# GpSimd's four-tap convolution in operations of 256 columns, two halves of each step in turn, on one Trainium2 core

## What is computed

```python
x = x + xattn(layernorm(x), ctx)            # one head over 8192 context rows, softmax
x = x + linear_attn(layernorm(x))           # 16 heads, relu features, rms norms
x = x + ffn(layernorm(x))
# ffn(h), h of 512 x 512
scores = sigmoid(h @ Wr)                    # router, 8 experts, the best 2 of scores + router_bias
cw = weights of the two chosen, normalised, zero elsewhere
hid = silu(h @ Wg[e]) * (h @ Wu[e])         # e = 0..3, 256 hidden columns each
routed = sum_e cw[:, e] * (hid @ Wd[e]) + (cw[:, 4] + cw[:, 6]) * h + cw[:, 7] * relu(h)
shared[t] = conv_b + sum_j conv_w[3 - j] * h[t - j]      # j = 0..3, per feature, causal
return routed + shared
```

## Time and profile before

| | |
|---|---|
| median of 3 runs | 528.38 us (528.27 to 528.65) |
| the profiled execution | 528.52 us, its span 526.4 us |
| outside the span | 2.1 us |
| granted TensorE clock | 0.999 of full speed |
| busy: PE, PEld | 521.2 us (99%), 433.2 us (82%) |
| busy: DVE, ACT, POOL | 373.4 us (71%), 243.8 us (46%), 244.1 us (46%) |
| the convolution on POOL | 464.8 to 517.2 us, 32 operations |

### The profile page before, as it was taken

The page is one execution under the profiler, slowest core; times in us unless marked ns, Lnnn a source line. Parts: engine busy times, 40 slices in busy tenths (PEclk is TensorE's granted clock), DMA queues, the critical chain, the costliest instruction groups (busy, mean ns, idle before and its releaser), DMA issues.

```text
span 526.4 us, 6975 instructions
## 1 busy us (share of the span) xinstructions
PE 521.2 (99%) x2524; PEld 433.2 (82%) x2524; DVE 373.4 (71%) x620; ACT 243.8 (46%) x391; POOL 244.1 (46%) x159
## 2 busy tenths in 40 slices
PE   9999999999999999999999999999999999999997
PEld 8888888888888888888888888888888888888785
DVE  5573768866668776466878544999967367649995
ACT  5743434745445454453545444656555332562210
POOL 3725006331211312234144342348529939897992
PEclk9999999999999999999999999999999999999999
DMA  8821223332422233422332212242340304741102
GB/s 290 331 69 52 80 95 106 113 127 82 158 82 80 81 105 136 157 85 80 122 119 80 82 40 82 80 161 90 113 157 1 127 34 136 244 162 60 60 1 80
DMA packets 17607, 57.10 MB, mean 108 GB/s; under 512 B 2083, under 2 KB 2595, under 8 KB 16806
## 3 DMA queue, kind: packets, MB, share of 16 engines
q1 hardware_dynamic: 17430, 56.53, 30.6%
q10 hardware_dynamic: 144, 0.13, 0.1%
HBM read 54.55 MB, written 2.10 MB: 108 GB/s over the span
## 4 chain that ended last, share of the span: by engine, by line
PE 95%; DVE 3%; issue 1%; ACT 0%; POOL 0%; DVEq 0%; POOLq 0%
PE bank L1459 24%; PE bank L1577 11%; PE bank L1588 11%; PE bank L1578 11%; PE bank L1589 11%; PE bank L1590 11%; PE bank L1579 11%; PE bank L1509 2%; PE bank L1449 1%; DVE tied L1362 1%; PE bank L1718 1%; PE bank L1470 1%; DVE xs L1398 1%; PE bank L1484 0%; DVE hid_l L1384 0%
## 5 line engine op out<-in xcount | busy, mean ns | idle before, releaser
L576 POOL TENSOR_TENSOR cn_l<-raw_n,cn_h 128x1024 fp32r<-128x1024 f32 x32 | 77.7, 2427 | 185.5 <-ACT cn_h L758 185.5
L776 ACT COPY ring<-bank 128x512 f32<-128x512 f32 x64 | 37.7, 589 | 148.3 <-PE bank L1579 148.0
L1093 DVE TENSOR_TENSOR top<-top,bank 128x512 f32<-128x512 f32 x60 | 41.1, 686 | 86.3 <-ACT ring L776 86.3
L1577 PE MATMUL bank<-qk_h,ct_h 128*128 128x512 f32 x256 | 99.8, 390 | 0.0
L1579 PE MATMUL bank<-qk_h,ct_l 128*128 128x512 f32 x256 | 99.6, 389 | 0.0
L1578 PE MATMUL bank<-qk_l,ct_h 128*128 128x512 f32 x256 | 99.6, 389 | 0.0
L1588 PE MATMUL bank<-ph,cn_h 128*128 128x512 f32 x256 | 99.6, 389 | 0.0
L1589 PE MATMUL bank<-pl,cn_h 128*128 128x512 f32 x256 | 99.6, 389 | 0.0
L1590 PE MATMUL bank<-ph,cn_l 128*128 128x512 f32 x256 | 99.6, 389 | 0.0
L1577 PEld LDWEIGHTS bank<-qk_h,ct_h 128*128 128x128 f32 x256 | 48.0, 188 | 10.7 <-issue 0.8
L1590 PEld LDWEIGHTS bank<-ph,cn_l 128*128 128x128 f32 x256 | 48.1, 188 | 10.1
(11 more groups left out here) (247 smaller groups left out, 906.3 us busy)
## 6 DMA issues: line engine op xcount, KB each, us to landing
raw_t<-ctx_t SPq DMA_DIRECT2D x32, 512.0 KB, 4.2
raw_n<-ctx_n SPq DMA_DIRECT2D x32, 512.0 KB, 3.3
piece_raw<-pieces SPq DMA_DIRECT2D x12, 512.0 KB, 3.3
shifted<-xn_rows SPq DMA_DIRECT2D x12, 256.0 KB, 3.1
taps<-taps_in SPq DMA_DIRECT2D x1, 1280.0 KB, 7.3
xs<-x SPq DMA_DIRECT2D x4, 256.0 KB, 5.3
wq_raw<-wq_t SPq DMA_DIRECT2D x4, 256.0 KB, 6.3
wk_raw<-wk_in SPq DMA_DIRECT2D x1, 1024.0 KB, 8.1
```

The source lines that it names most:

```text
L576: pool.tensor_tensor(cn[p % CNB][1][:], raw_n[p % 2][:], cn[p % CNB][0][:].bitcast(F32), ALU.subtract).then_inc(cnl_ready, 1)
L1093: dve.tensor_tensor(top[:], top[:], bank[:, S_BANKS[i % 2], :], ALU.max).then_inc(max_done, 1)
L1577: pe.matmul(bank[:, dst, :], ct[i // 2 % 2][0][:, c, keys], qk[0][:, c, :], start=(c == 0), stop=False)
```

## The change

Each of the eight steps of a token tile becomes two operations of 128x256, the left half of the columns and then the right half. `conv_chain` is replaced by `chain_last`: every operation but the last two of a tile still counts in `conv_step`, but the engine waits only after the right half. So a left half waits for both halves of the step before, and a right half waits for nothing. The last right half of a tile raises `conv_ready`, as the whole operation did. The 32 operations become 64. No other engine's list changes.

```diff
-            def conv_chain(ins):
+            def chain_last(ins, part):
                 ins.then_inc(conv_step, 1)
                 steps[0] += 1
-                pool.wait_ge(conv_step, steps[0])
+                if part.start > 0:
+                    pool.wait_ge(conv_step, steps[0])
...
-                conv_chain(pool.tensor_tensor(conv[:, t, :], xn[:, t, :], taps[:, PAD, :], ALU.mult))
-                conv_chain(pool.tensor_tensor(conv[:, t, :], conv[:, t, :], taps[:, TAPS, :], ALU.add))
+                parts = [slice(h * HALF, (h + 1) * HALF) for h in range(2)]
+                for part in parts:
+                    chain_last(pool.tensor_tensor(conv[:, t, part], xn[:, t, part], taps[:, PAD, part], ALU.mult), part)
+                for part in parts:
+                    chain_last(pool.tensor_tensor(conv[:, t, part], conv[:, t, part], taps[:, TAPS, part], ALU.add), part)
...
                 for j in range(1, TAPS):
-                    conv_chain(pool.tensor_tensor(tap_term[:], shifted[t % 2][:, j - 1, :], taps[:, PAD - j, :], ALU.mult))
-                    ins = pool.tensor_tensor(conv[:, t, :], conv[:, t, :], tap_term[:], ALU.add)
-                    if j < PAD:
-                        conv_chain(ins)
+                    for part in parts:
+                        chain_last(pool.tensor_tensor(tap_term[:, part], shifted[t % 2][:, j - 1, part], taps[:, PAD - j, part],
+                                                      ALU.mult), part)
+                    for part in parts:
+                        ins = pool.tensor_tensor(conv[:, t, part], conv[:, t, part], tap_term[:, part], ALU.add)
+                        if j < PAD:
+                            chain_last(ins, part)
                 ins.then_inc(conv_ready, 1)
```

## The result

| | before | after |
|---|---|---|
| median of 6 runs | 528.42 us | 530.39 us (529.48 to 530.86) |
| profiled execution, its span | 528.52, 526.4 us | 530.41, 528.6 us |
| time outside the span | 2.1 us | 1.8 us |
| last addition of VectorE ends | 523.90 us | 526.03 us |
| the convolution on GpSimd | 464.79 to 517.21 | 464.47 to 522.67 |

The changed kernel takes 1.0038 of the time before, 95% interval 1.0028 to 1.0048: **slower by 2.0 us**, where 1.8 was forecast.

What follows compares the result with a forecast made beforehand. TensorE bounds the kernel, with GpSimd's convolution 3.24 us inside its slack; in halves it ends at 522.1, past 520.45. The sum gave +1.7, the walk +1.9; taken +1.8: 528.52 + 1.8 = 530.3 us, range 528.0 to 532.8.

Steps and rivals of the forecast that it cites:

- A half operation: GpSimd's two-input operation on 256 columns: 0.74 us, of which 0.19 is a fixed part; ends 0.65 and 0.80.
- B: Rival: the fixed part overlaps, an undisturbed step in halves costs under 1.45 us, giving 527.8 us; chance 0.13.
- D: Rival: a half costs more, 0.80 us, making a step 1.64 and the time 533.2 us; chance 0.12.
- The boundaries: Between GpSimd operations: 0.08 us after a wait, 0.04 overlap without; an undisturbed step goes from 1.37 to 1.52 us.
- Turns of VectorE: VectorE operations with both inputs in SBUF hold up GpSimd's convolution: 18 turns of 0.38 us, mean of 0.32 and 0.44.
- Rival C: VectorE gets in only where GpSimd waits on its semaphore; turns cost 0.32 us, time 529.2 us; chance 0.10.
- The router: Its small compares on VectorE before tile 1: 0.5 us earlier to 0.6 later, taken as no change; weights ready at 479.0.
- Tiles 1 to 3: The convolution on GpSimd after the pause: 42.9 us from 479.2, so it ends at 522.1.
- The walk through all five lists: Following all five engines' lists through the stretch with the same rule: +1.9 us, half a microsecond either way.
- The slack: The convolution may end as late as 520.45 without delaying the final additions; it ended 3.24 us ahead of that.
- TensorE's stall: TensorE's idle 0.70 us before 490.21, waiting for VectorE's sum of expert 0; forecast to go.
- The end: VectorE's last addition: 522.1 + 0.03 + 0.71 + 2.71 = 525.6 against 523.90, +1.7 us.

## Why the prediction was right, step by step

- **A half operation.** Taken as 0.74: measured 0.740 and 0.744 in the median. Rivals B and D fall with it, and the experiment in quarters shows why: the fixed part of 0.19 us stays at 128 columns.
- **The boundaries.** Forecast 1.52 us a step: measured 1.51 to 1.52. Without the wait it is 1.39, where the sum of the parts has 0.70 + 0.70 = 1.40.
- **Turns of VectorE.** 18 forecast and 18 found: 11 in tile 1, 4 in tile 2, 3 in tile 3, counting the pairs that run over 1.44 by one or two turns. Their size was off. I took the mean of 0.32 and 0.44, and the pairs' excess adds up to 7.5 us, 0.42 a turn. There are two reasons: 10 of the 18 fell between two halves, where a turn costs 0.44 to 0.46, and three of the 8 at an end with a wait cost 0.44, 0.44 and 0.53, not 0.32. The 1272 ns in the line of L646 is the last of these. That is 0.7 us of the difference. Why these three were longer is open. Removing eight turns gave 0.40 each.
- **Rival C** is wrong for this kernel, since VectorE does get in between halves. The passing over in one profiled execution of another kernel shows that it can fail to.
- **The router** ended where it had, at 478.94 against 478.89, as taken: waits of at most 0.6 us at the compares, against two later operations now disturbed, 0.85 and 0.85. Tile 1 began at 479.08 (479.2 forecast).
- **Tiles 1 to 3** took 43.6 us against 42.9 in the sum, the turns' 0.7. The walk through all five lists had allowed for where each turn falls. It had 1.9 for the whole, and was nearer than the sum.
- **The slack** of 3.24 us: two more whole steps (2.7 us) were free, four cost 1.9 us. The sum counts the hand-over of 0.03 twice, and from the convolution's last addition to the final four is 0.61 us where it has 0.68 and 0.03; the slack was about 0.1 larger.
- **TensorE's stall** went, as forecast, and was worth nothing in the changed kernel because the convolution set the end. Taking it as 0.70 was too much: that is the largest of four executions in which it could arise, and the others have 0.08, 0.22 and 0.33. Where it is gone and the convolution ends in time, the median span is 0.1 to 0.45 shorter.
- **The end.** 526.03 against 525.55 in the sum: the convolution ended 0.57 later than its 522.1 (the turns' 0.7 less 0.12 of the start), and VectorE went from its addition to the final four in 0.61 us, not 0.71. The span grew by 2.2 us, the time of the profiled execution by 1.9.
- **What was luck.** The mechanism was right and the closeness of the number was partly luck. The last addition came 2.1 us later, against 1.7 in the sum and 1.9 in the walk, because turns were priced too low. The forecast added its difference in the span to the whole time and so took the time outside the span as unchanged. That fell by 0.3 us, which hid most of the miss.

## What to carry to other kernels

An engine that carries none of the last chain can still be near its end: work out how late its last result may come before cutting its work into smaller pieces, since each piece adds its fixed part (here 0.15 us in each step on GpSimd), and VectorE's turns between two halves cost more (0.44 to 0.46 us against 0.32). Cut only where somebody waits: one tile in halves freed TensorE's stall, and the other three only spent slack. When two halves are meant to hide each other's completion, each must wait for its own half, not for both: that alone took back 1.9 of the 2.0 us. And before a gain of half a microsecond is credited to a change, see whether it lies in the span, and whether the wait that it is to remove is as long in a second execution.

## What the runs showed that was not expected

In one profiled execution of the kernel in which each half waits only for its own half, a VectorE operation with both inputs in SBUF was passed over at four ends of GpSimd operations in a row and took 3.55 us; in a second profiled execution of the same program it took 0.91. In the first one itself other operations of VectorE had got in at such ends. A list of GpSimd operations in which no wait holds the engine up can thus now and then shut VectorE out, here at a cost of 1.7 us of idle time on TensorE. What decides it was not tried.

The time outside the span fell from about 2.1 us to about 1.8 in every kernel whose GpSimd list differs from that of the kernel before (1.9 with two more steps), and stayed at 2.1 where only VectorE's terms were shortened. What it comes from was not tried either.
